# A graph network on one core: some gathered columns are fetched by SyncE row by row, others are built by TensorE

## The reference

```
def _gat_layer(x, src, dst, W, a_s, a_d, b, num_nodes):
    h = (x @ W).reshape(num_nodes, H, C)
    alpha_src = einsum('nhc,hc->nh', h, a_s); alpha_dst = einsum('nhc,hc->nh', h, a_d)
    e = leaky_relu(alpha_src[src] + alpha_dst[dst], 0.2)
    e = exp(e - segment_max(e, dst)[dst])
    alpha = e / segment_sum(e, dst)[dst]
    msg = h[src] * alpha[:, :, None]
    return segment_sum(msg, dst).reshape(num_nodes, H * C) + b
```

## Time and profile before

| | |
|---|---|
| median of 3 runs | 6570.73 us (6566.15 to 6571.8) |
| span of the profiled execution | 6570.3 us |
| instructions | 37,158 |
| VectorE busy | 4654.6 us (71%) |
| GpSimd busy | 4293.2 us (65%) |
| ScalarE busy | 1375.2 us (21%) |
| TensorE busy | 1251.3 us (19%) |
| gathers of line 725 | 3,136, 953 ns each |

### The profile page before, as it was taken

One profiled execution on the slowest core, in us unless ns is written; L12 is line 12 of the kernel. 1 busy time (PEld: TensorE's weight loads), 2 busy tenths in 40 slices (PEclk: granted clock), 3 DMA queues, 4 the chain that ended last, 5 costly groups with the idle time before them and its releaser, 6 DMA issues. The chain is left out here.

```text
span 6570.3 us, 37158 instructions
## 1 busy us (share of the span) xinstructions
PE 1251.3 (19%) x8049; PEld 1094.3 (17%) x8049; DVE 4654.6 (71%) x9455; ACT 1375.2 (21%) x3580; POOL 4293.2 (65%) x4445
## 2 busy tenths in 40 slices
PE   7100000145555534332000000810000010000000
PEld 6100000135544433322000000610000010000000
DVE  7788888799999969987888887744444444444445
ACT  0122222220111114431000000622222211222223
POOL 0777777667777760027777775367777767777775
PEclk9555555555555555556555555955555555555555
DMA  9666666433443437754666664123333323333332
GB/s 391 199 218 202 202 199 204 130 106 131 132 136 133 133 115 292 295 184 153 220 219 218 225 218 158 30 85 109 113 111 109 115 74 90 112 113 109 113 111 82
DMA packets 338944, 1032.97 MB, mean 157 GB/s; under 512 B 100325, under 2 KB 163137, under 8 KB 331294
## 3 DMA queue, kind: packets, MB, share of 16 engines
q0 software_dynamic: 166752, 401.68, 21.4%
q1 hardware_dynamic: 116642, 342.34, 14.8%
q10 hardware_dynamic: 55324, 286.57, 12.1%
HBM read 602.97 MB, written 427.39 MB: 157 GB/s over the span
## 5 line engine op out<-in xcount | busy, mean ns | idle before, releaser
L725 POOL DMA_INDIRECT rows<-table,idx x3136 | 2987.4, 953 | 985.0 <-issue 973.1
L644 POOL DMA_INDIRECT by_src<-ebuf,place x784 | 767.4, 979 | 275.0 <-issue 238.3
L1296 DVE SCALAR_TENSOR_TENSOR psA<-psA,cont,dstf 128x128 f32<-128x128 f32 (+1 forms) x2349 | 836.6, 356 | 48.0 <-ACT ebuf L1025 27.2
L1285 DVE TENSOR_TENSOR sc<-rows,ebuf 128x56 f32<-128x56 f32 x112 | 28.2, 252 | 1023.9 <-DMA rows<-table,idx 1023.9
L958 PE MATMUL psA<-dstf,ones 128*128 128x512 f32 x10 | 9.9, 1113 | 3055.3 <-DVE dstf L2223 3055.3
L1296 DVE SCALAR_TENSOR_TENSOR sums<-sums,cont,psA 128x128 f32<-128x128 f32 (+1 forms) x1512 | 518.9, 343 | 30.3 <-ACT psA L1221 29.0
L958 PEld LDWEIGHTS psA<-dstf,ones 128*128 128x128 f32 x10 | 2.7, 317 | 3056.9 <-issue 3056.9
L823 PE MATMUL psA<-attr,sums 128*128 128x49 f32 x1568 | 406.1, 403 | 470.8 <-DVE attr L1475 470.8
L2104 DVE TENSOR_TENSOR_SCAN psA<-rows,psA 128x1980 f32<-128x1980 f32 x112 | 480.0, 4286 | 3.9
L823 PEld LDWEIGHTS psA<-attr,sums 128*128 128x128 f32 x1568 | 397.0, 326 | 476.9 <-DVE attr L1475 476.9
L1227 ACT ACTIVATE psA<-df 128x60 f32<-128x60 f32 (+1 forms) x168 | 40.4, 241 | 1714.2 <-DVE df L1285 1714.2
(11 more groups left out here) (350 smaller groups left out, 5533.6 us busy)
## 6 DMA issues: line engine op xcount, KB each, us to landing
dstf<-spread_wide SPq DMA_DIRECT2D x168, 924.0 KB
states<-sums ACTq DMA_DIRECT2D x150, 952.0 KB, 4.0
rows<-by_src SPq DMA_DIRECT2D x55, 1035.0 KB, 5.1
states<-sums ACTq DMA_DIRECT2D x56, 1008.0 KB, 5.7
spread_wide<-sums SPq DMA_DIRECT2D x56, 924.0 KB, 24.7
states<-sums ACTq DMA_DIRECT2D x56, 903.0 KB, 7.4
rows<-table,idx POOLq DMA_INDIRECT x3136
msg<-low_rows SPq DMA_DIRECT2D x56, 448.0 KB, 3.7
```

Source lines behind the costliest of these rows:

```text
L644: pool.indirect_dma_start(by_src[:, :], bass.IndirectOffsetOnAxis(ap=place[:, s, j:j + 1], axis=0), payload[:, s, j, :], None).then_inc(so ...
L725: pool.indirect_dma_start(rows[:, at:at + GW[ph]], None, table[ph][:, :], bass.IndirectOffsetOnAxis(ap=idx[:, s, j:j + 1], axis=0)).then_i ...
L1285: return dve.tensor_tensor(o_, a_, b_, op)
L1296: return dve.scalar_tensor_tensor(o_, a_, s_, b_, op0, op1)
```

## The change

Two groups of columns are no longer gathered by GpSimd.

First, in turn 54 (`SIDE`) of every walk SyncE fetches the first 10 columns (walks 0 and 2) or 12 columns (GAT walks). For each of the 128 partitions it loads 10 or 12 node numbers from `src` into registers and issues one DMA per number, one table row into one partition of a tile of its own. GpSimd gathers the other 4 or 2 columns of that turn into the same tile. That makes 1,280 or 1,536 DMAs a walk. In the GAT walks they are issued in one run, in walks 0 and 2 in 52 portions behind the dst loads of turns 1 to 52. Turn 54 leaves `rows`' slots, so turn 55 uses slot 0.

Second, in the GAT walks, odd turns 3 to 53 are marked (26 a walk). Their last column is not gathered. VectorE writes the column's node numbers on a diagonal, TensorE spreads them to all partitions (`wanted_by_all`), and VectorE compares them with the node numbers of each of the 49 blocks, 7 blocks at a time: 7 masks of 128x896 in 4 buffers. TensorE multiplies each block's mask (128x128) with that block's 136 columns of `aux`, 49 matmuls summed in PSUM, which yields the 128 wanted table rows; ScalarE copies them into the slot with two activations. Masks 0 to 3 of turn g are made after turn g-2's scan, masks 4 to 6 after turn g-1's.

Also, ScalarE's copies to `idx` are gone: gathers take their index from `src`. `aux` gets four more columns (one small copy per table group in phases 3 and 4), some semaphores are merged, and one tile of the phase 1 sort moves from `ebuf` to `msg`.

```diff
+SIDE = 54
+SIDE_COLS = {0: 10, 2: 10, 3: 12, 4: 12}
...
+        side_tile = {0: ebuf, 2: aux[:, :, :].rearrange("p b d -> p (b d)"), 3: msg, 4: msg}
...
+        def row_slot(ph, g):
+
+            side = SIDE if ph in SIDE_COLS else NG
+            return None if g == side else (g - int(g > side)) % 2
+
+        def marked(ph, g):
+
+            return ph >= 3 and 3 <= g < NG and row_slot(ph, g) == 1
...
+            def side_open(ph):
+
+                sp.wait_ge(src_in, 48)
+                if ph == 0:
+                    sp.wait_ge(chains_ready, 1)
+                    sp.wait_ge(bias3_ready, 1)
+                    for k in range(2):
+                        sp.wait_ge(tab_first[k], 16 * -(-(KG - k) // 2))
+                else:
+                    sp.wait_ge(tab_saved, 16 * KG * TURN[ph])
+                    sp.wait_ge(n_kept, (2 if ph == 2 else 3) * KG)
+
+            def side_rows(ph, parts):
+
+                w, at, n = GW[ph], SIDE * B, SIDE_COLS[ph]
+                for p in parts:
+                    sp.load(numbers_of[0:n], src[p:p + 1, at:at + n])
+                    for j in range(n):
+                        node = sp.snap(numbers_of[j])
+                        sp.dma_start(side_tile[ph][p:p + 1, j * w:(j + 1) * w], table[ph][bass.ds(node, 1), :]).then_inc(side_landed[ph], 16)
...
                 if ZW[ph] == 4:
                     sp.dma_start(dflat[:, 0:CH * 4], view.rearrange("p c d -> p (c d)")).then_inc(slim_in, 16)
+                    if ph in SIDE_COLS:
+                        side_open(ph)
+                        side_rows(ph, range(P))
...
+                        if ph in SIDE_COLS and g == 1:
+                            side_open(ph)
+                        if ph in SIDE_COLS and 1 <= g < SIDE - 1:
+                            side_rows(ph, range((g - 1) * P // (SIDE - 2), g * P // (SIDE - 2)))
...
-                    for it in range(IT):
-                        for s in range(2):
-                            g = it * 2 + s
-                            pool.wait_ge(idx_staged, g + (1 + TURN[ph] * (NG + 2)))
-                            pool.wait_ge(rows_used, g + (1 + TURN[ph] * NG))
-                            if g == 1 and ph < 3:
-                                spreads_landed()
-                            for j in range(B):
-                                at = (s * B + j) * GW[ph]
-                                pool.indirect_dma_start(rows[:, at:at + GW[ph]], None, table[ph][:, :],
-                                                        bass.IndirectOffsetOnAxis(ap=idx[:, s, j:j + 1], axis=0)).then_inc(rows_landed[s], 16)
+                    pool.wait_ge(src_in, 48)
+                    if ph:
+                        pool.wait_ge(n_kept, (2 if ph == 2 else 3) * KG)
+                    for g in range(NG):
+                        s = row_slot(ph, g)
+                        if s is None:
+                            for j in range(SIDE_COLS[ph], B):
+                                pool.indirect_dma_start(side_tile[ph][:, j * GW[ph]:(j + 1) * GW[ph]], None, table[ph][:, :],
+                                                        bass.IndirectOffsetOnAxis(ap=src[:, g * B + j:g * B + j + 1], axis=0)).then_inc(side_gathered, 16)
+                            continue
+                        pool.wait_ge(rows_used, free_at(ph, g))
+                        if g == 1 and ph < 3:
+                            spreads_landed()
+                        for j in range(B - int(marked(ph, g))):
+                            at = (s * B + j) * GW[ph]
+                            pool.indirect_dma_start(rows[:, at:at + GW[ph]], None, table[ph][:, :],
+                                                    bass.IndirectOffsetOnAxis(ap=src[:, g * B + j:g * B + j + 1], axis=0)).then_inc(rows_landed[s], 16)
...
+                def marked_columns():
+
+                    pe.wait_ge(n_stage, KG * (ph + 1))
+                    if ph == 4:
+                        pe.wait_ge(own_kept, KG)
+                    for n in range(marked_turns(ph, 0), marked_turns(ph)):
+                        pe.wait_ge(marks_made, (KG + 1) * n + 1)
+                        pe.matmul(wanted_by_all, ones[:, :], wanted, start=True, stop=True).then_inc(marks_read, 1)
+                        pe.wait_ge(marked_out, n)
+                        for q in range(KG):
+                            pe.wait_ge(marks_made, (KG + 1) * n + q + 2)
+                            for b in range(KB):
+                                k = q * KB + b
+                                m = pe.matmul(marked_rows, marks[(KG * n + q) % NM][:, b, :], aux[:, k, :], start=k == 0, stop=k == NB - 1)
+                            m.then_inc(marks_read, 1)
...
+                def keep_marked(t):
+
+                    n = marked_turns(ph, t)
+                    row = turn_rows(ph, t)[:, B - 1, :]
+                    act.wait_ge(marks_read, (KG + 1) * (n + 1))
+                    act.wait_ge(rows_used, free_at(ph, t))
+                    act.activation(row[:, 0:132].rearrange("p (h d) -> p h d", h=4)[:, :, 0:32],
+                                   marked_rows[:, 0:D].rearrange("p (h d) -> p h d", h=4), ACT.Copy)
+                    act.activation(row[:, 132:136], marked_rows[:, 132:136], ACT.Copy).then_inc(marked_out, 1)
...
+                        link(cp(aux[:, grp(g), D + 4:D + 8], scores[:, :, 0:4]))
...
+                def ask_marked(t):
+
+                    ts(wanted, ident[:, :], columns[:, t // 2:t // 2 + 1], ALU.mult).then_inc(marks_made, 1)
+
+                def mark_nodes(t, parts):
+
+                    n = marked_turns(ph, t)
+                    if parts[0] == 0:
+                        dve.wait_ge(marks_read, (KG + 1) * n + 1)
+                        link(ts(apart, wanted_by_all, own_row, ALU.subtract))
+                    for q in parts:
+                        i = KG * n + q
+                        if i >= NM:
+                            dve.wait_ge(marks_read, (KG + 1) * ((i - NM) // KG) + (i - NM) % KG + 2)
+                        tt(marks[i % NM], apart.unsqueeze(1).to_broadcast([P, KB, P]),
+                           first_of[:, q * KB:(q + 1) * KB].unsqueeze(2).to_broadcast([P, KB, P]), ALU.is_equal).then_inc(marks_made, 1)
+
                 def turn(it, last):
                     for s in range(2):
                         g = it * 2 + s
+                        if marked(ph, g + 2):
+                            ask_marked(g + 2)
+                        if marked(ph, g):
+                            dve.wait_ge(marked_out, marked_turns(ph, g) + 1)
...
+                        if row_slot(ph, g) is None:
+                            dve.wait_ge(side_landed[ph], 16 * P * SIDE_COLS[ph])
+                            dve.wait_ge(side_gathered, side_gathered_at(ph))
+                        else:
+                            dve.wait_ge(rows_landed[row_slot(ph, g)], landed_at(ph, g))
...
                                 turned_messages(g, G3, Sp)
+                                if marked(ph, g + 2):
+                                    mark_nodes(g + 2, range(0, 4))
+                                if marked(ph, g + 1):
+                                    mark_nodes(g + 1, range(4, KG))
```

More of the change, by code:

```diff
@@ L97, in build @@
         aux = sb("aux", [P, NB, 136])
-        src = sb("src", [P, CH + 2 * B], I32)
+        src = sb("src", [P, CH], I32)
         cont = sb("cont", [P, CH])
@@ L251, in build @@
         ssums = [sums[:, 0:B * 136], sums[:, B * 136:2 * B * 136], dflat[:, 1792:1792 + B * 136]]
+        marks = [ebuf[:, 4 * CH + k * KB * P:4 * CH + (k + 1) * KB * P] for k in range(3)] + [aflat]
+        marks = [m.rearrange("p (b n) -> p b n", b=KB) for m in marks]
+        NM = len(marks)
+        wanted = digits[:, 0:P]
+        columns = wt[:, :, :].rearrange("p s b -> p (s b)")
+        first_of = indeg
+        own_row = cg[:, 0, 0:1]
+        side_tile = {0: ebuf, 2: aux[:, :, :].rearrange("p b d -> p (b d)"), 3: msg, 4: msg}
         psA = ctx.enter_context(nc.psum_tensor("psA", [P, 4096], F32))
@@ L263, in build @@
         chain_exq = psA[:, 2048:2048 + 4 * (B + 1)]
+        marked_rows = psA[:, 2560:2696]
+        wanted_by_all = psA[:, 3072:3072 + P]
+        apart = psA[:, 3072 + P:3072 + 2 * P]
         held = psA[:, 2048:2048 + B * D].rearrange("p (b d) -> p b d", d=D)
@@ L360, in build @@
         dve_step = sem("dve_step")
-        idx_staged = sem("idx_staged")
+        side_landed = {p: sem(f"side_landed{p}") for p in SIDE_COLS}
+        marks_made = sem("marks_made")
+        marks_read = sem("marks_read")
+        marked_out = sem("marked_out")
+        side_gathered = sem("side_gathered")
         rows_landed = [sem(f"rows_landed{s}") for s in range(2)]
@@ L439, in scattered_at, with marked_turns, slot_columns, landed_at @@
             return 16 * KB * (ph * turns + g // ZS + 1)
+        def row_slot(ph, g):
[3 more added lines that the diff above has]
```

(37 more changed lines are left out.)

36 lines of the change are left out of this document (16 added, 20 removed).

## The result

The changed kernel takes 6459.34 us (median of 4 runs, 6458.45 to 6459.99), the kernel before 6570.01 (4 runs, 6566.15 to 6571.8). The ratio is 0.9835, with a 95% interval of 0.9823 to 0.9846: 111 us or 1.65% faster. The profiled execution has a span of 6458.2 us, against 6570.3 before, so the two profiles differ by 112.1 us and that difference can be taken apart stretch by stretch.

What follows compares the result with a forecast made beforehand. GpSimd's back-to-back gathers were taken to bound the GAT walks, with VectorE finishing last in walks 0 and 2. Terms -95.6 - 8.9 + 2 = -102.5 us took 6570.73 to 6468 us, range 6445 to 6545.

Steps and rivals of the forecast that it cites:

- GAT walks: Walks 3 and 4: 38 fewer GpSimd gathers each at 1.2575 us, 47.8 us a walk, 95.6 us saved in both.
- walks 0 and 2: Turn 54 moves up only by its wait for rows, 4.54 and 4.41 us: 8.9 us saved together, not 25.
- index copies: Removing 224 ScalarE copies: at most 4 x 0.2 us in walk 0, counted as 0.
- score copies and the rest: Extra score copy per table group in phases 3 and 4: 2 us added, 1.6 of it in phase 3.
- The third rival: Walks 0 and 2 give their full gather saving of 25 us: 16 us more gain, 6452 us; chance 0.06.
- SyncE's row: One partition's register load and 12 DMAs for turn 54: 3.3 to 9.5 us, taken as 6.6, costing nothing.
- The allowed 7.28: GAT walks: SyncE's time per row of 12, in us, below which turn 54 does not wait (932/128).
- The first rival: SyncE is late for turn 54: 6651 us at 8.0 us a row, 7330 at 9.5; chance 0.16.
- TensorE's column: Marked GAT turns: masks, 49 matmuls and copy stay hidden; TensorE some 12 to 24.8 us, VectorE up to 4.3 late.
- the second rival: GAT walks: TensorE stays at half clock, mark loop takes 35.2 us against 33.9; 33 us a walk, 6534; chance 0.12.
- Added on the path: Extra score copies in phases 3 and 4 add 2 us; set-up operations lie under the first turn's gathers.

Runs made afterwards that it cites:

- experiment 1: Changed kernel with both column groups given back to GpSimd, gathers still indexed from src without the copies: 6572.55 us, ratio 1.0003 to the kernel before.
- experiment 4: Changed kernel with SyncE's columns in the GAT walks alone, none in walks 0 and 2, TensorE's columns kept: 6473.32 us, ratio 0.9849 to the kernel before.
- experiment 3: Changed kernel with SyncE's columns alone, no turn marked for TensorE: 6531.9 us, ratio 0.9939 to the kernel before.
- experiment 7: Changed kernel with SyncE fetching all 14 columns of turn 54 in the GAT walks, GpSimd none: 6653.02 us, ratio 1.0114 to the kernel before.
- experiment 5: Changed kernel with the last column of marked turns neither gathered nor made by TensorE: 6463.01 us, ratio 0.9826 to the kernel before.
- Experiment 6: Changed kernel with each matmul of a marked column done a second time into unread PSUM: 6576.98 us, ratio 0.9998 to the kernel before.
- experiment 2: Changed kernel with TensorE's columns alone, turns 3 to 53 marked and no SyncE columns: 6500.01 us, ratio 0.9892 to the kernel before.
- experiment 8: Changed kernel with SyncE fetching 13 columns of turn 54 in the GAT walks, GpSimd one: 6480.47 us, ratio 0.9855 to the kernel before.

## Why the prediction was right

The forecast was 6468 in a range of 6445 to 6545, the result 6459.34. Its mechanism held: GpSimd's back-to-back gathers set the GAT walks, 38 fewer shorten each, and everything added hides beside them. The terms, by the profiled spans:

| term | predicted | measured |
|---|---|---|
| GAT walks | -95.6 | -51.4 - 50.8 = -102.2 |
| walks 0 and 2 | -8.9 | -10.0 - 3.1 = -13.1 |
| index copies | 0 | none seen (experiment 1: ratio 1.0003, +2 us, within its interval) |
| score copies and the rest | +2 | +3.2, the remainder |
| sum | -102.5 | -112.1 |

*GAT walks: mis-sized by 6.6 us.* 38 x 1.2575 = 47.8 used the mean period of a walk. That mean holds six gaps of about 0.75 us. Without gaps it is 933.5/745 = 1.253 (744 gathers and the two of turn 54), and 38 of those are 47.6. My sum left the gaps where they were, and they went: six of 0.75 us are 4.5 more, 52.1 together, where the walks show 51.4 and 50.8.

*Walks 0 and 2: mis-sized by 4.2 us.* In walk 0 VectorE begins turn 55 at 1226.54, 1006.7 us after the first gather, against 1238.20 - 221.5 = 1016.7 before:

```profile
1209.80 2.02 DVE L1398 TENSOR_TENSOR ebuf<-psA,ebuf 128x1792 f32<-128x1792 f32 x1
...
1226.54 2.03 DVE L1398 TENSOR_TENSOR rows<-psA,rows 128x1792 f32<-128x1792 f32 x1
```

Turn 54 starts with no idle, as said, 9.6 us earlier and not 4.54, since turn 53 itself began 5.1 us earlier. The prediction had put GpSimd's waits for a free slot in walk 0 (9.5 us in 4 places) at nothing. Four of about 2.4 us each stood before; of those the last two, 686 and 852 us after the first gather, are gone, which is 4 of the 5.1 us. GpSimd's slot waits in walk 0 of the changed kernel, then of experiment 4:

```profile
  ACT psA L1334: 5.4, 4
```

```profile
  ACT psA L1334: 8.5, 5
```

They are 8.7 us in experiment 1, also without SyncE's rows in walk 0, and 5.4 in experiment 3, with them. So they are shorter where SyncE's rows run in walk 0, and removing the index copies alone leaves most of them; by which path, no run settled. In walk 2 the turns start so:

```profile
4007.83 2.02 DVE L1398 TENSOR_TENSOR rows<-rows,psA 128x1792 f32<-128x1792 f32 x1 [1.80 <-DMA rows<-table,src]
...
4023.79 2.02 DVE L1398 TENSOR_TENSOR aux<-aux,psA 128x1792 f32<-128x1792 f32 x1
...
4039.75 2.02 DVE L1398 TENSOR_TENSOR rows<-rows,psA 128x1792 f32<-128x1792 f32 x1
```

Turn 55 begins 986.0 us after the first gather, 989.1 before: 3.1 of the 4.41. The wait that went is the one that was named, and the rest of GpSimd's saving is lost to VectorE's own 15.96 us a turn, as the prediction had it. The third rival, all 25 us, is out.

*SyncE's row: right for the wrong parts.* 6.6 us predicted, 6.61 measured. But the load was taken at 1.9 and takes 1.03, and a DMA with its two register instructions was taken at 0.39 and takes (6.61 - 1.03)/12 = 0.465. The two errors cancel at 12 columns: by the same parts a row of 13 is 6.97 us and one of 14 7.36, and they measured 7.30 and 8.02. That the figure came out to 0.01 us is luck. The allowed 7.28 is 7.23. The first rival's figure, 6651 at 8.0 us a row, was met by experiment 7: 8.02 us and 6653 (6645 by the ratio). So this rival was the right one to fear, its margin on the ordinary chip was 0.6 us a row, and on the other chip SyncE is late.
The Trainium skill (Runtime: NRT & Kernel Launch, section Instruction fetch mechanics) has about 200 ns per register, which would be 2.4 us for 12, an estimate; the trace shows 1.03, 86 ns per register. The page tells of loads from HBM, and this one reads SBUF. The measurement decides.

*TensorE's column.* Parts 4 to 6 were to take 5.3 to 10.6 us and take 8.0; VectorE was to begin a marked turn up to 4.3 us after its rows land; experiment 5 puts this at 1.4 us for turn 53, with no effect on GpSimd. (The 5.6 us of the wait are another thing, VectorE's idle time since its last mask, which it would otherwise spend waiting for gathered rows: 7.99 us before turn 53 in experiment 5.) The whole column costs TensorE 853.6 us for 52, 16.4 each, between the 12 and 24.8 of the two clocks:

```profile
L1050 PE MATMUL psA<-aux,ebuf 128*128 128x136 f32 x3822 | 636.1, 339 | 702.2 <-DVE ebuf L1398 702.2
...
L1050 PE MATMUL psA<-aux,attr 128*128 128x136 f32 x1274 | 217.5, 337 | 227.3 <-DVE attr L1398 227.3
```

So the second rival fell because the clock rises within each stream, 3.54 to 1.78 us for 14 records, with a mean of 0.73 over the 200 us of the windows. By that, the Trainium skill's rule (TensorE: Matmul & The Clock Gate, section Part 1), throttled by default and released by sustained activity, agrees with the trace. Experiment 6 shows that the rival's loop exists: with 11.2 us of wait per marked turn GpSimd runs out of buffers. The prediction gave it 0.12, with 24.8 us of TensorE a column at the half clock; with about 25.6 us, from twice the work, it is there. Its price was put at 33 us a walk and is 55.9: 43.0 in GpSimd's queue and 12.9 at the walk's end, which the prediction had left out.

*Added on the path.* 3.4 us stand between the last turn of walk 3 and the first gather of walk 4 (5407.9 - 5247.02 = 160.9; 157.5 before). I had counted the copies of phase 4 as mostly hidden and put most of 2 us in phase 3. It is the other way round: from turn 55 of walk 2 to walk 3's first gather it is 271.1 us, 272.0 before (268.3 and 268.2 in experiments 1 and 2, without SyncE's rows; why, no run settled). Of the 3.4 us, 1.6 are also in experiment 1 (159.1), with neither group, so they belong to what it keeps, such as the score copies. The other 1.8 appear in the runs with both groups (160.7 to 161.2 in experiments 4, 6, 7 and 8) and not in those with one alone or with the column not made (158.8 to 159.2 in 2, 3 and 5). By which path, no run settled.

## What to carry to other kernels

Find the engine that issues back to back and count what its queue loses; work moved from it to engines with slack is worth its full period there, however clumsy the substitute (16.4 us of TensorE for one gather of 1.25 us), until a loop through the new wait closes. Where a second queue takes over part of the work, work out the price per item at which it becomes late, measure one size more, and keep a margin: 6.61 us a row was free, 7.30 cost 8 us a walk, 8.02 cost 99. A kernel whose margin lies in the rate at which one engine issues instructions should be timed on more than one chip.

## What the hardware showed that I had not expected

- SyncE's register load from SBUF grows faster than its registers: medians of 1.03 us for 12, 1.26 for 13 and 1.46 for 14. With 10, in walks 0 and 2, it is 1.24, more than with 12. Those walks have more DMA traffic (share 0.62 against 0.38); whether that is the reason, no run settled.
- The gap of about 0.75 us every 126 gathers, which goes away when turns of 14 and 13 gathers alternate.
- One chip on which the kernel before takes 7514 us, SyncE's rows of 12 take 13.2 us in place of 6.61 with the same medians of load and DMA, and TensorE's matmuls start 2 to 3 us apart in stretches for no reason that the profile names. The four kernels with SyncE's rows that ran there are 20 to 23% slower there than the kernel before.
- The granted clock doesn't follow the busy share alone: 0.73 at 94 busy us of 200 in streams of float32 matmuls with 136 columns, 0.50 at 156 of 300 in the rank stretch.
